# First key chunk of a masked cross attention: f32 products of unscaled operands in place of scaled f16 parts, with the scale work laid between the first steps

## The reference, cut to what matters

```python
Q = (query @ W_q).reshape(b, m, H, D_K).transpose(0, 2, 1, 3)
K = (key_value @ W_k).reshape(b, n, H, D_K).transpose(0, 2, 1, 3)
V = (key_value @ W_v).reshape(b, n, H, D_V).transpose(0, 2, 1, 3)
scores = jnp.einsum('bhmk,bhnk->bhmn', Q, K)
scores = jnp.where(mask == 0, jnp.float32(-1e+20), scores)
attn = jax.nn.softmax(scores / np.sqrt(D_K).astype(np.float32), axis=-1)
ctx = jnp.einsum('bhmn,bhnv->bhmv', attn, V)
return ctx.transpose(0, 2, 1, 3).reshape(b, m, H * D_V) @ W_o
```

## Time and profile before

| | us |
|---|---|
| median of 3 runs | 411.26 (410.97 to 412.98) |
| span of the profiled execution | 411.3 |
| PE busy | 383.6 (93%) |
| DVE busy | 292.4 (71%) |
| ACT busy | 287.4 (70%) |
| POOL busy | 223.7 (54%) |

### The profile page before, as it was taken

How to read it: one execution, slowest core, us unless ns; L and a number is a source line. 1 busy time by engine, 2 the same in 40 slices (tenths; PEclk the granted TensorE clock), 3 DMA queues, 4 the chain that set the end, 5 groups by cost and what they waited for, 6 DMA issues and landing times.

```text
span 411.3 us, 11571 instructions
## 1 busy us (share of the span) xinstructions
PE 383.6 (93%) x4620; PEld 297.5 (72%) x4620; DVE 292.4 (71%) x762; ACT 287.4 (70%) x568; POOL 223.7 (54%) x163
## 2 busy tenths in 40 slices
PE   6988999999999999987989999999999999999986
PEld 3445777777767778876966767777777779878875
DVE  2788888888776777666767767988787777454543
ACT  3477888888886887646439988889988877352330
POOL 2397989999974653001007896877887551020010
PEclk9899999999999999999999999999999999999988
DMA  8899997989999989980006999999999999500000
GB/s 309 313 253 157 210 179 133 181 145 215 229 172 229 194 180 158 386 345 0 3 2 104 184 177 225 191 194 190 196 200 181 191 195 207 228 3 3 2 2 3
DMA packets 188390, 68.56 MB, mean 167 GB/s; under 512 B 183200, under 2 KB 183984, under 8 KB 187440
## 3 DMA queue, kind: packets, MB, share of 16 engines
q1 hardware_dynamic: 188048, 66.77, 81.2%
q10 hardware_dynamic: 288, 1.05, 0.7%
HBM read 21.90 MB, written 0.03 MB: 53 GB/s over the span
## 4 chain that ended last, share of the span: by engine, by line
PE 43%; DVE 22%; DMA 10%; ACT 9%; POOL 8%; issue 7%; SPq 1%; DVEq 0%; POOLq 0%; ACTq 0%
PE ps L521 15%; PE ps L489 11%; DVE probs L628 10%; DMA probsT<-halves 8%; POOL halves L591 5%; ACT probs L558 3%; ACT halves L565 2%; PE ps L763 2%; PE ps L1091 2%; DVE probsT L657 2%; DMA moe<-in_ctxT 2%; PE ps L501 2%; DVE U L646 1%; DVE halves L591 1%; PE ps L1198 1%
## 5 line engine op out<-in xcount | busy, mean ns | idle before, releaser
L591 POOL TENSOR_TENSOR halves<-probs,halves 128x896 f16<-128x896 f32 x75 | 141.6, 1892 | 62.7 <-ACT halves L565 61.4
L521 PE MATMUL ps<-ctxN,probsT 128*128 128x128 f16 x2352 | 148.9, 219 | 4.7 <-DMA probsT<-halves 4.3
L521 PEld LDWEIGHTS ps<-ctxN,probsT 128*128 128x128 f16 x2352 | 139.4, 98 | 18.8 <-issue 6.7
L489 PE MATMUL ps<-ctxT_parts,GT_parts 128*128 128x512 f16 (+1 forms) x660 | 143.0, 353 | 6.7 <-DVE negmax L628 6.5
L558 ACT ACTIVATE probs<-probs,shifted 128x896 f32<-128x896 f32 x112 | 115.5, 1031 | 7.3 <-DVE shifted L633 7.3
L489 PEld LDWEIGHTS ps<-ctxT_parts,GT_parts 128*128 128x128 f16 x660 | 59.4, 98 | 56.3 <-DVE negmax L628 9.0
L565 ACT CAST halves<-probs 128x896 f16<-128x896 f32 x93 | 85.8, 922 | 0.0
L646 DVE SCALAR_TENSOR_TENSOR U<-U,alpha,ps 128x128 f32<-128x128 f32 x112 | 38.5, 343 | 51.9 <-PE ps L521 51.6
L628 DVE CUSTOM_DVE_ANT_0 probs<-ps,zero,negmax 128x896 f32<-128x896 f32 x56 | 67.4, 1204 | 2.0 <-POOL halves L591 1.6
L628 DVE CUSTOM_DVE_ANT_0 probs<-ps,maskb,negmax 128x896 f32<-128x896 f32 x56 | 67.4, 1204 | 1.6 <-issue 0.7
L555 ACT ACTIVATE alpha<-negmax 128x1 f32<-128x1 f32 x96 | 28.2, 294 | 39.5 <-DVE negmax L628 38.5
(11 more groups left out here) (365 smaller groups left out, 375.0 us busy)
## 6 DMA issues: line engine op xcount, KB each, us to landing
moe<-in_ctxT SPq DMA_DIRECT2D x7, 448.0 KB, 7.8
moe<-in_mask SPq DMA_DIRECT2D x6, 448.0 KB, 10.5
moe<-in_gateT SPq DMA_DIRECT2D x2, 1024.0 KB, 9.4
moe<-in_upT SPq DMA_DIRECT2D x2, 1024.0 KB, 10.7
moe<-in_downT SPq DMA_DIRECT2D x2, 1024.0 KB, 12.6
moe<-in_fir_long SPq DMA_DIRECT2D x1, 2048.0 KB, 10.2
probsT<-halves SPq DMA_TRANSPOSE x93, 4.7
wv<-in_wv SPq DMA_DIRECT2D x2, 512.0 KB, 6.1
```

The source lines that it names most:

```text
L489: ins = pe.matmul(ps[:, 2 * b + h, 0:width], GT_parts[:, g_part, r * P:(r + 1) * P], ctxT_parts[:, keys:keys + width], start=(g_part == 0 ...
L521: ins = pe.matmul(ps[:, bank, 0:D], probsT_parts[:, b, p_part, k * P:(k + 1) * P], ctxN_parts[:, at:at + D], start=(p_part == 0 and c_part ...
L591: eng.tensor_tensor(halves_of(L, n)[:, 1, :], probs[:, n % BUFS, :], halves_of(L, n)[:, 0, :], ALU.subtract).then_inc(lower_of(L, n)[0], 1)
```

## The change

Chunk 0 is no longer split for its scores. Its 8 score tiles are each two f32 products, of the raw context with an unscaled f32 copy of G (`G32`, which lies in the storage of `UT`). They need neither scale nor bound, so the loop can start once G is copied. The f16 parts of chunk 0's context are still made, since the turned context needs them, and the f16 parts of G are needed from step 8 on. All the scale work is laid between the first steps:

- DVE, behind maximum(2) to maximum(7) (`SCALES_AT`): two channel maxima and the scales; the lower context parts; the bound; the scale of G; the two halves of G's lower part.
- ACT: three channel sums before exps(0), one behind upper(0); the upper context parts behind exps(2); the whole upper part of G (1024 wide) behind exps(6).
- POOL: mask 0 whole, then the parts of chunk 1, the power and mask 1 behind steps 0 to 3 (`FIRST_AT`); mask 1 also waits for `g_scale`, since it uses a masked value scaled by the bound.
- PE: the two runs of 10 and 11 filling products are gone; the small product for the bound stands behind score(5); score(8) waits for the third count of `g_copied`, which is the second half of G's lower part.
- SP: mask 0 is loaded right behind chunk 0 of the context; masks 4, 5 and 6, the parameters and the second part of the constants move between the turning DMAs of steps 3, 6, 10 and 8; the first `turn_ctx` stands behind that of step 0.

Some semaphores of the later self attention are merged under one name, with the same waits.

```diff
-MASKED = -1e20
+MASKED = -1e35
+BOUND_FLOOR = (2.0 ** -20, 2.0 ** -60)
+FIRST_AT = {0: 0, 1: 1, 2: 2, 3: 3}
+SCALES_AT = {2: 0, 3: 1, 4: 2, 5: 3, 6: 4, 7: 5}
+CTX_FIRST_AT, G_PARTS_AT = 2, 6
+BOUND_AT = 3
+MASK_LOADS_AT, CST_AT, TURN_FIRST_AT = {3: 4, 6: 5}, 8, 0
...
+        G32 = UT[:].rearrange("p r c -> p (r c)")
...
             for n in range(STEPS):
                 turn(0, n)
+                if n == RT + 2:
+                    sp.wait_ge(sem("scores_ready"), RT)
+                    sp.wait_ge(sem("g_upper"), 2)
+                    sp.wait_ge(sem("g_copied"), G_COPIED[0] + 2)
+                    load_mask(MASK_SLOTS)
                 if n % RT == 3 and n // RT + 1 < CH:
                     turn_ctx(n // RT + 1)
+                if n == TURN_FIRST_AT:
+                    turn_ctx(0)
+                if n in MASK_LOADS_AT:
+                    load_mask(MASK_LOADS_AT[n])
+                if n == CST_AT:
+                    load("par", par[:], "par")
...
-                if n == RT // 2:
+                if n == (RT if L == 0 else RT // 2):
                     pe.wait_ge(sem("g_copied"), G_COPIED[L + 1] - 1)
...
+                if L == 0 and c == 0:
+                    if n == 0:
+                        pe.wait_ge(sem("g_first"), 1)
+                        pe.wait_ge(sem("ld_ctxT0"), 16)
+                    if n == RT // 2:
+                        pe.wait_ge(sem("g_upper"), 1)
+                    for h, (at, width) in halves_at:
+                        ins = pe.matmul(ps[:, 2 * b + h, 0:width], G32[:, r * P:(r + 1) * P],
+                                        ctxT_raw[:, at:at + width], start=True, stop=True)
+                    ins.then_inc(sem("scores_ready"), 1)
+                    return
...
+                if L == 0 and i == BOUND_AT:
+                    pe.wait_ge(sem("squares"), 2)
+                    pe.matmul(ps[:, 4, 0:3], C("ones"), squares[:, 0:3], start=True,
+                              stop=True).then_inc(sem("bound_summed"), 1)
...
                 if i == 0:
-                    g_upper_act(act, L)
+                    if L:
+                        g_upper_act(act, L)
                     upper(0)
-                if 2 <= i <= STEPS and not on_pe(L, i - 1):
+                    if L == 0:
+                        channel_sum_act(act, CH - 1)
+                if L == 0 and i == 1:
+                    upper(1)
+                if L == 0 and i == CTX_FIRST_AT:
+                    ctxT_first_act(act)
+                if L == 0 and i == G_PARTS_AT:
+                    act.wait_ge(sem("g_scale"), 1)
+                    act.wait_ge(sem("g_first"), 1)
+                    act.wait_ge(sem("g_copied"), G_COPIED[0])
+                    act.activation(GT_parts[:, 0, :], G32, ACT.Copy, scale=g_scale[:, 0:1]).then_inc(sem("g_upper"), 1)
+                if 3 - L <= i <= STEPS and not on_pe(L, i - 1):
                     upper(i - 1)
...
         def fold_q_dve(dve, seq, i):
             if i == 0:
-                channel_max_dve(dve, (0,))
+                channel_max_dve(dve, 0)
...
-                channel_max_dve(dve, (2, 3, 4, 6))
-                channel_scales_dve(dve, seq)
-                dve.wait_ge(sem("bound_summed"), 1)
-                bound_dve(dve, seq, 0, ps[:, 7, 2 * D:2 * D + 3])
-                ctxT_first_dve(dve, 0)
-                ctxT_first_dve(dve, 1)
-            if i < 2:
+                dve.wait_ge(sem("g_ready"), 1)
+                dve.tensor_copy(G32[:, 0:P], ps[:, 6, 0:P]).then_inc(sem("g_first"), 1)
+                dve.wait_ge(sem("g_ready"), 2)
+                dve.tensor_copy(G32[:, P:4 * P], ps[:, 4, P:4 * P]).then_inc(sem("g_copied"), 1)
+                channel_max_dve(dve, 2)
+                return
+            if i == 1:
...
+        def first_scales_dve(dve, seq, part):
+
+            if part == 0:
+                channel_max_dve(dve, 5)
+                channel_max_dve(dve, CH - 1)
+                channel_scales_dve(dve, seq)
+            if part == 1:
+                ctxT_first_dve(dve, 0)
+                ctxT_first_dve(dve, 1)
+            if part == 2:
+                dve.wait_ge(sem("bound_summed"), 1)
+                bound_dve(dve, seq, 0, ps[:, 4, 0:3])
+            if part == 3:
+                descale_dve(dve, seq, 0, scale_g_dve(dve, seq, 0))
+            if part > 3:
+                cols = slice((part - 4) * 4 * P, (part - 3) * 4 * P)
+                dve.wait_ge(sem("g_upper"), 2)
+                dve.scalar_tensor_tensor(GT_parts[:, 1, cols], G32[:, cols], g_scale[:, 0:1], GT_parts[:, 0, cols],
+                                         ALU.mult, ALU.subtract).then_inc(sem("g_copied"), 1)
...
-            keep_busy(pe, 11)
             flash_pe(pe, 0)
...
             def mask(c):
                 pool.wait_ge(sem(f"ld_mask{c}"), 16)
+                if c == 1:
+                    pool.wait_ge(sem("g_scale"), 1)
...
+            mask(0)
+            pool.wait_ge(sem("ch_scale"), 1)
             for n in range(STEPS):
                 if not on_pe(0, n) and not on_vector(0, n):
                     lower(pool, 0, n)
                 denominators(pool, 0, n)
-                if n == 0:
-                    mask(1)
+                if n in FIRST_AT:
+                    (partial(ctxT_upper, 1), partial(ctxT_lower, 1), partial(bound_pool, pool, 0), partial(mask, 1))[FIRST_AT[n]]()
...
-            flash_dve(dve, 0, {1: partial(g_lower_dve, dve, 0, slice(4 * P, 8 * P), 5)})
+            flash_dve(dve, 0, {n: partial(first_scales_dve, dve, seq, part) for n, part in SCALES_AT.items()})
```

More of the change, by code:

```diff
@@ L425, in _ @@
                 sp.dma_start(ctxT_raw[:, keys], dram["ctxT"][:, keys]).then_inc(sem(f"ld_ctxT{c}"), 16)
-            for c in range(4):
+                if c == 0:
+                    load_mask(0)
+            for c in range(1, 4):
                 load_mask(c)
[L428 to L432, removed]
             for n in range(STEPS):
                 turn(0, n)
+                if n == RT + 2:
[3 more added lines that the diff above has]
+                    load_mask(MASK_SLOTS)
                 if n % RT == 3 and n // RT + 1 < CH:
                     turn_ctx(n // RT + 1)
+                if n == TURN_FIRST_AT:
[4 more added lines that the diff above has]
+                    load("par", par[:], "par")
+                    sp.dma_start(cst[:, first:], dram["cst"][:, first:]).then_inc(sem("ld_par"), 16)
                 if n in WEIGHTS_AT:
@@ L628, in maximum @@
                 dve.tensor_tensor_reduce(out=probs[:, n % BUFS, :], in0=scored, in1=added,
-                                         scale=descale[:, L:L + 1], scalar=negmax[:, n:n + 1], op0=ALU.add,
+                                         scale=descale[:, 2:3] if L == 0 and n < RT else descale[:, L:L + 1], scalar=negmax[:, n:n + 1], op0=ALU.add,
                                          op1=ALU.min, accum_out=negmax[:, n + RT:n + RT + 1]).then_inc(
@@ L702, in ctxT_first_dve @@
             keys = FIRST_KEYS[half]
[L703 to L705 removed]
+            ins = dve.scalar_tensor_tensor(ctxT_parts[:, CK + keys.start:CK + keys.stop], ctxT_raw[:, keys],
+                                           ch_scale[:], ctxT_parts[:, keys], ALU.mult, ALU.subtract)
+            if half:
+                ins.then_inc(sem("ctxT_ready"), 1)
         def bound_dve(dve, seq, L, total):
@@ L792, in fold_q_pe @@
                 loaded(pe, "wkT0")
-                for swap in range(2):
-                    for k in range(PAIRS // 2):
+                for swap, ks in ((0, (0,)), (1, range(PAIRS // 2)), (0, range(1, PAIRS // 2))):
+                    for k in ks:
                         for par_ in range(2):
@@ L882, in channel_sum_act, with ctxT_first_act @@
             keys = slice(c * CK + HALF if last else c * CK, (c + 1) * CK)
-            act.activation({1: probs[:, 0, :], 5: probsT[:, 0, :], 6: probs[:, 1, 0:HALF]}[c], ctxT_raw[:, keys], ACT.Abs,
+            act.activation(probsT[:, c % 4, 0:keys.stop - keys.start], ctxT_raw[:, keys], ACT.Abs,
                            accum_out=ch_amax[:, c + last:c + last + 1]).then_inc(sem("ch_max"), 1)
+        def ctxT_first_act(act):
+            act.wait_ge(sem("ch_scale"), 1)
+            for keys in FIRST_KEYS:
+                act.activation(ctxT_parts[:, keys], ctxT_raw[:, keys], ACT.Copy,
+                               scale=ch_scale[:]).then_inc(sem("ctxT_upper"), 1)
         def fold_q_act(act, i):
@@ L897, in fold_q_act @@
                                accum_out=squares[:, 1:2]).then_inc(sem("squares"), 1)
-                channel_sum_act(act, 5)
-                channel_sum_act(act, 6)
-                act.wait_ge(sem("ch_scale"), 1)
-                for keys in FIRST_KEYS:
-                    act.activation(ctxT_parts[:, keys], ctxT_raw[:, keys], ACT.Copy,
-                                   scale=ch_scale[:]).then_inc(sem("ctxT_upper"), 1)
+                channel_sum_act(act, 1)
+                act.wait_ge(sem("g_ready"), 2)
```

(6 more changed lines are left out.)

89 lines of the change are left out of this document (39 added, 50 removed).

## The result

The changed kernel took 416.08 us (median of 6 runs, 415.01 to 416.43), the kernel before 411.4 (6 runs, 410.62 to 413.76). The ratio is 1.0112, with an interval of 1.0083 to 1.0142. So the change costs 4.7 us, 1.1%; the forecast was 415.6.

What follows compares the result with a forecast made beforehand. The prediction took PE to bound the first attention loop from about score(10), with DVE, ACT and POOL setting the pace before; 411.3 + 2.3 (late score(10)) + 2.0 (clock) = 415.6 us, range 408.5 to 419.5.

Steps and rivals of the forecast that it cites:

- The early start: Start of kernel: f32 score tiles of 1.55 us let maximum(0) start at 13.6 instead of 21.10, 7.5 us early.
- The first chain: DVE, first steps: scales done at 20.7, lower(0) at 21.8, maximum(3) at 23.0, POOL's product held by lower(0).
- rival 2: POOL's product gets in before lower(0): score(10) +4.7 us, time 417.5 to 421; chance 0.15.
- The wait for the power: DVE after maximum(5): waits 1.2 us for POOL's power, which stands behind chunk 1's context remainder.
- DVE waits for ACT's part of G: DVE after maximum(6): waits 2.3 us for ACT's 1024-wide part of G, done at 35.7.
- The collision behind it: DVE before score(8): POOL's lower(4) holds maximum(7) to 38.4, part 5 ends at 39.0, score(8) starts at 39.1.
- The clock: PE idle 6.3 us before score(8), so the granted clock falls to half pace: +2.0 us, bounds 0 to 3.5.
- Loop at PE's pace: First attention loop from about score(10): PE sets the pace, so a later score(10) delays the kernel equally.
- The base: Starting time for the sum: 411.3 us, taken as span of the profiled execution and also the median.
- Rival 1: The forecast itself: score(8) late and the clock falls, 415.6 us, range 413.3 to 417.5; chance 0.45.
- Rival 3: No difference, 409.2 to 413.3 us: passes don't hold one another, score(8) at 36.0, score(10) at 40.6; chance 0.18.
- Rival 4: Faster, 408 us: DVE without a single wait, score(8) before 35, PE's gap under 2 us, score(10) at 38; chance 0.22.

Runs made afterwards that it cites:

- e5: Changed kernel with POOL's power set ahead of the context remainder of chunk 1; 414.34 us, ratio 1.0086 to the kernel before.
- e2: Changed kernel with ACT's upper part of G one step earlier, behind exps(5) instead of exps(6); 414.81 us, ratio 1.0101 to the kernel before.
- e1: Changed kernel with 20 filling products in PE's gap between pv(0) and score(8); 413.87 us, ratio 1.0078 to the kernel before.
- g3: g2 plus the power ahead of the context remainder on POOL, as in e5; 410.82 us, ratio 1.0001 to the kernel before.
- e4: Changed kernel with score(8) waiting only for the first half of G's lower part, score(12) for the second; 413.83 us, ratio 1.0083 to before.
- g2: g1 with the second half of G's lower part two steps later, behind maximum(9); 410.21 us, ratio 0.998 to the kernel before.
- e3: Changed kernel with G's lower parts read from PSUM for all but the first 128 columns; 415.8 us, ratio 1.0113 to the kernel before.
- g1: Changed kernel with the edits of e2 and e4 together; 411.28 us, ratio 1.0013 to the kernel before.

## Why the prediction was right

The side and the mechanism held, and the size came close: 4.3 us forecast, 4.7 measured. That it came so close is in part luck, since two terms missed in opposite directions. By its own steps:

- **The early start** (maximum(0) at 13.6, f32 tile 1.55): 14.01 and 1.60. Lead 7.1 us instead of 7.5.
- **The first chain** to the scales (20.7) and to maximum(3) (ends at 23.0): lower(0) started at 20.96 and maximum(3) with its bias ended at about 23.4. As said, lower(0) came just ahead of POOL's product, by 0.05 us, and the product was held to 2.58. The other order, rival 2's, was that close.
- **The wait for the power** (1.2 us of DVE) did not show as a wait. POOL's context remainder got in before lower(2) and held it to 2.74; the power was done at 30.3 and by then DVE was still in maximum(5). The same pass costs the time in another place, and e5 shows it: with the power ahead, lower(2) takes 1.08 and score(8) comes 2.0 earlier.
- **DVE waits for ACT's part of G,** 2.3 forecast, 2.24 measured. e2 takes it away, and score(8) moves by just that.
- **The collision behind it** is the step that was off. I had mask 1 on POOL from 33.1 to 36.3, so the first half of G's lower part would be free and the second held for 0.4. The mask ran 1 us earlier (32.16 to 35.44), lower(4) caught the first half, and that cost 1.47 (2.21 against 0.74), where 0.4 stood. So score(8) started at 40.18, not at 39.1, and this alone makes the lateness +3.4 at score(10), without the clock, where +2.3 stood.
- **The clock** was forecast at +2.0, measured at +1.57 in the profile and +1.4 in time by e1, which the intervals alone would not show. It was low for about 6.8 us, longer than I took, but half of that lay in the idle gap.
- **Sum at score(10):** 3.4 + 1.57 = 5.0 against 4.3: 1.1 too little for the collision, 0.4 too much for the clock.
- **Loop at PE's pace:** held. Score(10) to the value projection took 129.3 to 129.7 in after and in six of the eight experiments, over a range of 6 us in the start of score(10). It was 1.1 to 1.6 longer in g3 (130.9), where score(10) came earliest, and in e1 (130.8), where it did not; both have waits for turning DMAs.
- **The base:** "span of the profiled execution, also the median" was wrong. The time is the span plus about 1.8, so this execution has a time of about 413.1, near the slowest of the three (412.98), and a median execution has a span of about 409.6. The number survived by luck: a slow execution's span, 411.3, happens to equal the median time, 411.26, to which the change has to be added. The 2.1 us of DMA waits in the earlier trace rows belong to that execution; they were no room that a late start could use.

Rival 1 (the forecast) is what happened, in its own range. Rival 2's time did not come; score(8) at 40.18 lay about half way between the forecast's 39.1 and its 41.4. Rival 3's condition, passes that don't hold one another, is refuted by the rows of after. The Trainium skill (SBUF — State Buffer, section "Who interferes with whom") has the same exclusion for a DVE pass with two SBUF inputs beside any GpSimd pass that reads SBUF. POOL's lower(4), product and remainder agree (2.21, 2.58, 2.74). The mask pass from int32 to bf16 agrees only one way round: it held no DVE pass, since G's half inside it took 0.75, but in g3, where G's half (31.99 to 33.12) was there first, the mask pass from 32.55 took 3.73 instead of 3.28. Where they differ, the measurement decides.

Rival 4, faster, needs more said, since its list of DVE's work was sound: g3 meets its condition (score(8) before 35, gap under 2 us) and still gives no 408. The lead at maximum(0) is 7.1 us, but the DVE and POOL work that stood ahead of the loop now stands inside it, ahead of maximum(8). In g3 POOL's list is the longer, and of the lead 1.9 us is left at score(10), with no fall of the clock on the way. That g3's loop took 1.2 to 1.6 us longer and that it has DMA waits is shown; that these waits come from the masks, parameters and constants that now run among the turning DMAs was not tried, and before, which has the longest such wait, speaks against it as the only source. No version here beats the kernel before by more than the measurement can tell.

What stays open: in e2, e4 and e5 the medians fell by 0.9 to 1.2 us less than score(10) moved in the one profiled execution of each. Where the low clock falls differs between executions, and that is a likely reason; only one execution of each was profiled, so it isn't shown. The rest of the kernel blurs the comparison as well: the stretch behind the loop differs by up to 2.2 us between profiled executions.

## What to carry to other kernels

Work that is taken out of a serial start and laid between the first steps of a loop isn't free because the bottleneck engine idles there: list each of the other engines' passes up to the first step at the bottleneck's pace, and see whether the lead outlasts the list. When two engines exclude each other, sub-microsecond shifts decide which pass is held, so price a hold at the full length of the other pass on the late chain, not at the overlap that one layout gives. A semaphore that covers two halves should be waited for by half: here that and one part moved up a step, which change no work, brought 4 us back (ratio 1.0112 to 1.0013). And before a start in one profile is read as the effect of an edit, look where the clock was low in that profile: g2 and g3 differ by 1.9 us at score(10) and by nothing measurable in time.

## What the runs showed of the hardware

- A hold is not scaled by the work of the held pass: 128 columns took 1.80 us beside POOL's lower, 512 columns 2.21, and a pass of one column on POOL, the power, 1.42 beside DVE's lower(2) where its like took 0.55 late in the same profile (204.82). In e3, passes that read one source from PSUM took 0.60 (384 columns, beside POOL's product) and 0.74 (512, beside its cast); the cast took 0.93, as it does alone.
- POOL's mask pass (int32 to bf16, 3.28 us) held no two-source pass of DVE: 0.75 for 512 columns in e2, e5, g1 and g2. But it was held itself where such a pass had begun first: 3.73 in g3.
- An f32 score tile, 896 columns in two products, takes 1.60 us from start to start at the full clock (three in 4.79) and 2.93 with the clock at 0.50 for all but the first 0.3 us (31.60 to 34.53 in e1); the six f16 products of a later tile take 1.13 (40.73 to 41.86).
- After 2.6 us of idle PE (34.0 to 36.6) the granted clock went to 0.50 for 6.8 us; with PE busy on 20 small f32 products it stayed at 1.00 from 36 on. The mean granted clock of the runs parts in the same way: 0.984 to 0.987 in the five kernels in which PE stood idle for 3.9 to 6.2 us ahead of score(8) (after, e2 to e5), 0.993 to 0.996 in the five others.
- The clock also fell with PE at work and no gap over 2.4 us behind it: at 31.4 to 32.4 us, in the last f32 tile, in e1, e3, g1 and g2, and not in after, e2 and e4, which have the same gaps there.
